# A fused attention and gate network on one core: the raw logits change PSUM banks, and the steps get a new order

## The chip, the cores and the metric

One core of a Trainium2 chip runs the whole program. Its engines are TensorE (PE, with its weight loads as PEld), VectorE (DVE), ScalarE (ACT) and GpSimd (POOL); SyncE (SP) issues nearly all DMAs. The metric is the device time of one execution in microseconds, as the median of several runs.

## The reference, cut to what matters

The input is x, 16 batches of 512 tokens with 256 features, layer-normalised to xn. Two networks read xn and their results are multiplied:

```
s = talking_heads_attention(xn)      # 16 heads of 16; logits mixed over heads before and
                                     # after the softmax
g = silu(local_gate(xn))             # 2 layers: windowed attention with 8 heads of 64,
                                     # window 128, then layernorm, gated gelu MLP
out = x + s * g

logits = einsum('bhid,bhjd->bhij', q, k) * SCALE     # the "raw" logits
logits = einsum('bhij,gh->bgij', logits, Wpre)       # the "mixed" logits
attn   = softmax(logits)
attn   = einsum('bhij,gh->bgij', attn, Wpost)
out    = einsum('bhij,bhjd->bhid', attn, v)
```

All of it is float32; the products of the gate are split in a high and a low part (three matmuls for one).

## The kernel before, in words

The program is a list of steps. `program()` (L242) strings together `AHEAD` (work for batch 0), then for each batch the text `ORDER` (L126; `FIRST_ORDER` and `LAST_ORDER` for the first and last), and each engine walks through that one list in `Counts.run` (L561), doing its own part of each step and waiting on semaphores for the others. Every engine therefore works strictly in the written order: an instruction that waits holds all that is written behind it on its engine.

Two strands share the list. The **talking-heads strand** goes, per batch:

- `raw.n.c` (32 a batch: 4 query tiles n, 8 pairs of heads c). TensorE multiplies queries by keys, one matmul into each of two banks (L963). ACT copies both banks to `raw_sb` (L1282), which has two slots and waits for the DMA of two steps before. SP waits for both copies and stores the slot in `raw_all` in DRAM (L714). The last c of a tile also issues the loads of the next queries.
- `scores.m` (32 a batch). TensorE mixes the heads of 16 query rows, read back through `raw_mix` (3 slots), into S0 and S1 (L975). DVE takes the maximum of each bank (L1547) and ACT the exponential (L1290). SP then loads a later `raw_mix`.
- `mixers.m`, `mix.m`, `values.c`, `project.t`: row sums inverted, the second mixing into M0 and M1, copies by ACT and DVE (`store_mixed`, L583), the product with the values and the output projection.
- `talk_q`, `talk_k`, `talk_v`: the projections of the next batch, in S0 and S1.

The **gate strand** goes, twice a batch: `x_turn`, `qkv` (banks F0, F1, F2), `q_turn` (F3) and `k_turn` (M1), 8 times `local_scores` (F0, F1), `weigh`, `p_turn` (F2, F3) and `local_values` (M1), 4 times `out_proj` (F3), then `half_turn`, `shift_turn`, `h_turn`, six `up` with `hide`, and four `down` (F0 to F3).

PSUM has eight banks, S0, S1, M0, M1, F0 to F3, and `banks_of` (L254) says which a step fills. A counting loop over the list (L288) numbers the fillings of each bank; before a step fills a bank, TensorE waits until the bank's last filling is emptied:

```
for k in ("S0", "S1"):
    if now.was_filled(step, k):
        pe.wait_ge(emptied[k], now.fill(step, k) - 1)
```

In the kernel before, `raw`, `scores` and the three `talk` steps all use S0 and S1. The steps `w_1_hi`, `w_1_lo`, `w_2_lo`, `w_o_lo`, `qkv_hi`, `qkv_lo`, `heads_v`, `ropes` and `keys` are loads by SP alone.

Of the kernel before, what the change touches and what calls it, by code (L numbers as in the profile page):

```python
# [131 lines left out]
mix.4 weigh.0.3 sigmoid.3 local_values.0.1 p_turn.0.2 mixers.6 silu gated qkv_hi.1 scores.7 mix.5 local_scores.0.5
weigh.0.4 out_proj.0.0 local_values.0.2 raw.2.1 mixers.7 p_turn.0.3 store local_scores.0.6 weigh.0.5 mix.6 scores.8
local_values.0.3 weigh.0.6 p_turn.0.4 raw.2.2 mixers.8 mix.7 raw.2.3 out_proj.0.1 local_values.0.4 w_1_hi.0 p_turn.0.5
raw.2.4 local_scores.0.7 local_values.0.5 values.1 p_turn.0.6 weigh.0.7 scores.9 mix.8 out_proj.0.2 local_values.0.6
raw.2.5 p_turn.0.7 raw.2.6 local_values.0.7 mixers.9 scores.10 out_proj.0.3 mix.9 half_turn.0 mixers.10 scores.11
# [5 lines left out]
join.1.3 q_turn.1.2 raw.3.6 k_turn.1.2 x_turn.0 ropes mix.16 scores.18 q_turn.1.3 k_turn.1.3 mixers.17 mixers.18
project.1 talk_k local_scores.1.0 scores.19 mix.17 local_scores.1.1 scores.20 weigh.1.0 mix.18 weigh.1.1 mixers.19
raw.3.7 split_k local_scores.1.2 w_o_lo.0 mix.19 p_turn.1.0 local_scores.1.3 weigh.1.2 weigh.1.3 keys talk_q
p_turn.1.1 local_values.1.0 w_1_hi.1 values.4 mixers.20 local_values.1.1 scores.21 p_turn.1.2 mix.20 mixers.21
local_scores.1.4 scores.22 out_proj.1.0 weigh.1.4 local_values.1.2 split_q p_turn.1.3 mixers.22 scores.23 mix.21
local_scores.1.5 mix.22 mixers.23 weigh.1.5 p_turn.1.4 local_values.1.3 scores.24 local_scores.1.6 mix.23 out_proj.1.1
scores.25 weigh.1.6 p_turn.1.5 local_values.1.4 values.5 mixers.24 local_values.1.5 raw.0.0 mixers.25 local_scores.1.7
scores.26 mix.24 out_proj.1.2 weigh.1.7 raw.0.1 p_turn.1.6 raw.0.2 mix.25 raw.0.3 p_turn.1.7 local_values.1.6
scores.27 local_values.1.7 project.2 raw.0.4 mixers.26 out_proj.1.3 raw.0.5 w_1_lo.1 mixers.27 mix.26 half_turn.1  # L150
scores.28 shift_turn.1 mix.27 raw.0.6 raw.0.7 h_scale.1 values.6 mixers.28 scores.29 h_turn.1 scores.30 mixers.29
# [7 lines left out]
k_turn.0.1 raw.1.2 bound mixers.1 join.0.2 qkv.0.3 sigmoid.0 mix.0 raw.1.3 scores.2 q_turn.0.2 join.0.3 k_turn.0.2
raw.1.4 q_turn.0.3 k_turn.0.3 raw.1.5 mixers.2 mix.1 raw.1.6 local_scores.0.0 scores.3 weigh.0.0 local_scores.0.1  # L160
mix.2 scores.4 mixers.3 p_turn.0.0 raw.1.7 sigmoid.1 weigh.0.1 mixers.4 local_scores.0.2 scores.5 mix.3
local_scores.0.3 p_turn.0.1 sigmoid.2 weigh.0.2 local_values.0.0 values.0 raw.2.0 mixers.5 local_scores.0.4 scores.6
mix.4 weigh.0.3 sigmoid.3 local_values.0.1 p_turn.0.2 mixers.6 silu gated qkv_hi.1 scores.7 mix.5 local_scores.0.5
weigh.0.4 out_proj.0.0 local_values.0.2 raw.2.1 mixers.7 p_turn.0.3 store local_scores.0.6 weigh.0.5 mix.6 scores.8
local_values.0.3 weigh.0.6 p_turn.0.4 raw.2.2 mixers.8 mix.7 raw.2.3 out_proj.0.1 local_values.0.4 w_1_hi.0 p_turn.0.5
raw.2.4 local_scores.0.7 local_values.0.5 values.1 p_turn.0.6 weigh.0.7 scores.9 mix.8 out_proj.0.2 local_values.0.6
raw.2.5 p_turn.0.7 raw.2.6 local_values.0.7 mixers.9 scores.10 out_proj.0.3 mix.9 half_turn.0 mixers.10 scores.11
w_1_lo.0 shift_turn.0 mixers.11 mix.10 w_2_lo.0 scores.12 raw.2.7 h_scale.0 mix.11 h_turn.0 mixers.12 scores.13
project.0 up.0.0 up.0.1 raw.3.0 hide.0.0 hide.0.1 up.0.2 up.0.3 hide.0.2 hide.0.3 mixers.13 up.0.4 raw.3.1 up.0.5
raw.3.2 hide.0.5 hide.0.4 values.2 norm raw.3.3 mix.12 scores.14 scale mix.13 qkv_lo.0 down.0.0 down.0.1 scores.15  # L170
down.0.2 mixers.14 down.0.3 raw.3.4 x_turn.1 mix.14 mixers.15 scores.16 qkv.1.0 join.1.0 mix.15 qkv.1.1 mixers.16
scores.17 q_turn.1.0 k_turn.1.0 join.1.1 qkv.1.2 q_turn.1.1 k_turn.1.1 raw.3.5 join.1.2 qkv.1.3 heads_v values.3
join.1.3 q_turn.1.2 raw.3.6 k_turn.1.2 x_turn.0 ropes mix.16 scores.18 q_turn.1.3 k_turn.1.3 mixers.17 mixers.18
# [1845 lines left out]
```

## Time and profile before

| | us |
|---|---|
| median of 3 runs | 5281.58 |
| lowest and highest | 5248.23 and 5287.87 |
| the profiled execution | 5270.36 |
| span of its instructions | 5268.6 |
| busy: PE, PEld | 4501.8 (85%), 3376.1 (64%) |
| busy: ACT, DVE, POOL | 3361.2 (64%), 3139.3 (60%), 1772.8 (34%) |
| mean granted TensorE clock | 0.940 |
| DMA, share of 16 engines | 55.2% on SP's queue |

PE is busy when any matmul is in flight. The granted clock is 1 at 2.4 GHz and 0.5 at 1.2 GHz; a mean between the two is a mixture of stretches at either level. Idle time is put down to the engine and line whose semaphore ended it; "issue" means that nothing in the profile ended it. A batch starts about every 320 us from the second one on.

### The profile page before, as it was taken

How to read it: one execution, taken by the hardware profiler on the slowest of the kernel's cores; microseconds unless marked ns; L12 is line 12 of the kernel's file. 1: busy time of each engine (PE TensorE's matmuls, PEld its weight loads, DVE VectorE, ACT ScalarE, POOL GpSimd, SP SyncE). 2: the span in 40 equal slices, each digit the busy share in tenths (PEclk: the TensorE clock that was granted, in tenths of full speed). 3: DMA queues.
4: the chain of work that ended last, by engine and by line, in shares of the span. 5: the costliest groups of instructions: out<-in, count | busy, mean ns of one | idle time of the engine just before them, and what ended most of it. 6: DMA issues, size and time to landing. Idle time of an engine off the chain costs nothing. (4 is left out here: it accounts for less than half of the span.)

```text
span 5268.6 us, 184953 instructions
## 1 busy us (share of the span) xinstructions
PE 4501.8 (85%) x75160; PEld 3376.1 (64%) x75160; DVE 3139.3 (60%) x8220; ACT 3361.2 (64%) x8621; POOL 1772.8 (34%) x1069
## 2 busy tenths in 40 slices
PE   3888888889988888888889888888888889888897
PEld 2666666666666666666666666666666666666665
DVE  3566556665556665656666566655566656566565
ACT  2666667666666665666666676666666666666665
POOL 2232333433324342333423333333243423334232
PEclk7998999999999999999999999999999999999999
DMA  6555566655566565566555665655665555655552
GB/s 195 206 178 206 186 189 204 184 189 192 192 208 190 187 192 184 188 194 214 171 204 190 193 206 177 201 187 187 209 188 199 182 200 181 201 203 169 194 173 81
DMA packets 397527, 997.62 MB, mean 189 GB/s; under 512 B 36496, under 2 KB 103056, under 8 KB 395152
## 3 DMA queue, kind: packets, MB, share of 16 engines
q1 hardware_dynamic: 385888, 969.02, 55.2%
q0 software_dynamic: 10800, 16.78, 1.6%
q8 instruction: 604, 9.90, 0.8%
q14 instruction: 235, 1.93, 0.1%
HBM read 655.35 MB, written 338.69 MB: 189 GB/s over the span
## 5 line engine op out<-in xcount | busy, mean ns | idle before, releaser
L1302 ACT ACTIVATE probs<-bank_S,neg_max 128x512 f32<-128x512 f32 x1024 | 692.4, 681 | 588.6 <-DVE neg_max L1554 563.7
L1003 PEld LDWEIGHTS bank_M<-mixer_n,probs 64*64 64x64 f32 x32768 | 626.6, 145 | 300.6 <-issue 276.3
L1554 DVE TENSOR_REDUCE neg_max<-bank_S 128x1 f32<-128x512 f32 x1024 | 658.0, 684 | 252.9 <-PE bank_S L986 248.7
L1855 POOL TENSOR_TENSOR l_probs<-l_probs,l_inv 128x1024 f32<-128x1024 f32 (+1 forms) x256 | 428.7, 1680 | 1089.5 <-DVE l_inv L1661 1089.5
L1003 PE MATMUL bank_M<-mixer_n,probs 64*64 64x64 f32 x32768 | 664.6, 232 | 112.5 <-issue 61.6
L986 PE MATMUL bank_S<-raw_mix,w_pre 64*64 64x512 f32 x4096 | 613.4, 663 | 144.6 <-ACT raw_sb L1288 66.0
L1840 POOL TENSOR_TENSOR inv_norms<-norms_c,minus_half 128x16 f32<-128x16 f32 x128 | 417.3, 3260 | 893.4 <-DVE norms_c L1595 893.4
L1288 ACT ACTIVATE raw_sb<-bank_S 128x512 f32<-128x512 f32 x1024 | 556.5, 599 | 211.5 <-PE bank_S L972 138.1
L1367 ACT ACTIVATE l_probs<-l_probs,l_least 128x256 f32<-128x256 f32 (+1 forms) x1024 | 480.6, 473 | 99.6 <-DVE l_least L1641 98.2
L1861 POOL TENSOR_TENSOR hidden_lo<-shared,hidden_hi 128x512 fp32r<-128x512 f32 x192 | 243.8, 1287 | 824.1 <-ACT hidden_hi L1438 824.1
L972 PE MATMUL bank_S<-keys,queries 48*128 48x512 f32 x1024 | 268.5, 515 | 256.0 <-ACT probs L1302 141.0
L592 DVE COPY mixed<-bank_M 128x512 f32<-128x512 f32 x512 | 348.8, 681 | 226.2 <-PE bank_M L1003 225.2
L1641 DVE CUSTOM_DVE_ANT_0 l_probs<-bank_F,mask,inv_norms 128x256 f32<-128x256 f32 (+1 forms) x1024 | 402.7, 447 | 0.7 <-issue 0.7
L1310 ACT ACTIVATE mixer_n<-mixer,row_inv 128x64 f32<-128x64 f32 x1024 | 295.6, 343 | 119.5 <-DVE row_inv L1545 119.4
L1743 DVE SCALAR_TENSOR_TENSOR shared<-bank_F,b,shared 128x512 f32<-128x512 f32 x192 | 143.8, 749 | 377.6 <-ACT shared L1432 349.7
L592 ACT COPY mixed<-bank_M 128x512 f32<-128x512 f32 x512 | 296.5, 579 | 94.7 <-PE bank_M L1003 92.7
L972 PEld LDWEIGHTS bank_S<-keys,queries 48*128 48x128 f32 x1024 | 105.4, 191 | 367.5 <-ACT probs L1302 153.0
L1581 DVE TENSOR_TENSOR shared<-bank_F,rot 128x512 f32<-128x512 f32 x512 | 321.2, 683 | 20.8 <-PE bank_F L914 19.4
L1022 PE MATMUL bank_M<-mixed,v_heads 128*32 128x64 f32 x16384 | 286.8, 229 | 49.9 <-issue 39.3
L912 PE MATMUL bank_F<-w_qkv_hi,xT_hi 128*128 128x512 f32 x768 | 314.2, 409 | 6.4 <-DVE xT_lo L1514 5.2
L1115 PE MATMUL bank_M<-pT,att 128*64 128x128 f32 x3584 | 264.1, 287 | 60.7 <-DVE mixed L592 37.6
L1022 PEld LDWEIGHTS bank_M<-mixed,v_heads 128*32 128x32 f32 x16384 | 260.0, 116 | 84.0 <-issue 69.9
(161 smaller groups left out, 10317.7 us busy)
## 6 DMA issues: line engine op xcount, KB each, us to landing
raw_all<-raw_sb SPq DMA_DIRECT2D x512, 512.0 KB, 3.5
raw_mix<-raw_all SPq DMA_DIRECT2D x512, 512.0 KB, 4.5
w_qkv_lo<-split_qkv SPq DMA_DIRECT2D x60, 768.0 KB, 6.1
w_qkv_hi<-split_qkv SPq DMA_DIRECT2D x60, 768.0 KB, 7.1
w_hi<-split SPq DMA_DIRECT2D x60, 704.0 KB, 5.0
w_lo<-split SPq DMA_DIRECT2D x60, 704.0 KB, 6.5
queries<-spilled_q SPq DMA_DIRECT2D x384, 64.0 KB
keys<-spilled_k SPq DMA_DIRECT2D x96, 256.0 KB, 7.6
```

Of the source, the lines that this page charges most:

```text
L592: copy(to, bank[k][:].rearrange("p (t c i) -> p t c i", t=2, i=HI)).then_inc(emptied[k], 1)
L972: mm(bank[f"S{hp}"][:], queries[rows, c, :], keys[rows, c, :], start=True, stop=True)\
L986: last = mm(bank[f"S{r}"][half * (P // 2):(half + 1) * (P // 2), :], w_pre[rows, :], raw_mix[rows, slot, half, :], start=True, stop=True)
L1003: last = mm(bank[f"M{r}"][keys, at:at + GH * HI], probs[rows, (2 * m + t) % PB, j * P + keys.start:j * P + keys.stop], mixer_n[rows, m % 2 ...
L1022: last = mm(bank["M0"][PAD * q:PAD * (q + 1), r * CI:(r + 1) * CI], v_heads[:, now.b % 2, j, pair:pair + PAD], mixed[:, j, g, :], start=(j ...
L1288: fn(raw_sb[:, c % SB, hp, :], bank[f"S{hp}"][:], ACT.Copy).then_inc(emptied[f"S{hp}"], 1)
L1302: fn(probs[:, n % PB, :], bank[k][:], ACT.Exp, bias=neg_max[:, n % 2:n % 2 + 1], accum_out=row_sum[:, n % 4:n % 4 + 1]).then_inc(emptied[k ...
L1367: fn(l_probs[:, u % LB, j, lo:], l_probs[:, u % LB, j, lo:], ACT.Exp, scale=-1.0, bias=l_least[:, u % 2, j:j + 1], accum_out=l_sum[:, u % ...
L1554: v.tensor_reduce(neg_max[:, t:t + 1], bank[k][:], AX.X, ALU.max, negate=True)\
L1641: ins = v.tensor_tensor_reduce(l_probs[:, u % LB, j, lo:], bank[k][:, pair * 2 * P + lo:(pair + 1) * 2 * P], mask[:, lo:], inv_norms[:, t, ...
L1840: g.tensor_tensor(inv_norms[:, t, :], norms_c[:], minus_half[:], ALU.pow).then_inc(inv_norm_done, 1)
L1855: g.tensor_tensor(l_probs[:, u % LB, :, lo:], l_probs[:, u % LB, :, lo:], l_inv[:, u % 2, :, None].to_broadcast([P, 4, 2 * P - lo]), ALU.m ...
```

## The change

The step `raw` gets the banks F2 and F3 in place of S0 and S1; all waits, copies and the matmul's target follow. `scores` keeps S0 and S1. The three order texts are replaced by new ones with the same steps. No instruction's shape, no buffer in SBUF and no DMA changes.

```
 def banks_of(step):
     kind = step[0]
-    if kind in ("raw", "scores"):
+    if kind == "raw":
+        return ["F2", "F3"]
+    if kind == "scores":
         return ["S0", "S1"]
...
             def keys_in(step):      # and the same in split_q
-                    sp.wait_ge(filled["S1"], now.fill(("raw", TW - 1, HC8 - 1), "S1", ago=1))
+                    sp.wait_ge(filled["F3"], now.fill(("raw", TW - 1, HC8 - 1), "F3", ago=1))
...
             def raw(step, n, c):    # SP
-                for k in ("S0", "S1"):
+                for k in banks_of(step):
                     sp.wait_ge(emptied[k], now.fill(step, k))
...
             def raw(step, n, c):    # TensorE
-                for k in ("S0", "S1"):
+                for k in banks_of(step):
                     if now.was_filled(step, k):
                         pe.wait_ge(emptied[k], now.fill(step, k) - 1)
                 for hp in range(HP):
                     rows = slice(hp * SEEN, hp * SEEN + STACK)
-                    mm(bank[f"S{hp}"][:], queries[rows, c, :], keys[rows, c, :], start=True, stop=True)\
-                        .then_inc(filled[f"S{hp}"], 1)
+                    mm(bank[f"F{2 + hp}"][:], queries[rows, c, :], keys[rows, c, :], start=True, stop=True)\
+                        .then_inc(filled[f"F{2 + hp}"], 1)
...
             def raw(step, n, c):    # ACT
-                    act.wait_ge(filled[f"S{hp}"], now.fill(step, f"S{hp}"))
-                    fn(raw_sb[:, c % SB, hp, :], bank[f"S{hp}"][:], ACT.Copy).then_inc(emptied[f"S{hp}"], 1)
+                    act.wait_ge(filled[f"F{2 + hp}"], now.fill(step, f"F{2 + hp}"))
+                    fn(raw_sb[:, c % SB, hp, :], bank[f"F{2 + hp}"][:], ACT.Copy).then_inc(emptied[f"F{2 + hp}"], 1)
```

The order, cut to four pieces of `ORDER` (old above new): the first windows of layer 0, the scaling of its hidden layer, the start of layer 1, and the `up` steps of layer 1.

```
-scores.0 qkv.0.0 join.0.0 scores.1 qkv.0.1 join.0.1 mixers.0 q_turn.0.0 k_turn.0.0 raw.1.0 qkv.0.2 raw.1.1 q_turn.0.1
-k_turn.0.1 raw.1.2 bound mixers.1 join.0.2 qkv.0.3 sigmoid.0 mix.0 raw.1.3 scores.2 q_turn.0.2 join.0.3 k_turn.0.2
+scores.0 raw.1.0 qkv.0.0 mixers.0 join.0.0 scores.1 raw.1.1 qkv.0.1 k_turn.0.0 q_turn.0.0 scores.2 join.0.1 raw.1.2
+mixers.1 mix.0 qkv.0.2 q_turn.0.1 mixers.2 k_turn.0.1 join.0.2 raw.1.3 scores.3 mix.1 raw.1.4 mixers.3 qkv.0.3
...
-w_1_lo.0 shift_turn.0 mixers.11 mix.10 w_2_lo.0 scores.12 raw.2.7 h_scale.0 mix.11 h_turn.0 mixers.12 scores.13
+out_proj.0.2 local_values.0.6 p_turn.0.7 local_values.0.7 scores.11 out_proj.0.3 half_turn.0 raw.2.5 mixers.10
+shift_turn.0 raw.2.6 w_1_lo.0 scores.12 mixers.11 h_scale.0 w_2_lo.0 mix.10 raw.2.7 h_turn.0 mix.11 mixers.12
...
-down.0.2 mixers.14 down.0.3 raw.3.4 x_turn.1 mix.14 mixers.15 scores.16 qkv.1.0 join.1.0 mix.15 qkv.1.1 mixers.16
+down.0.3 mix.14 x_turn.1 scores.16 raw.3.1 mixers.15 qkv.1.0 join.1.0 mix.15 raw.3.2 scores.17 qkv.1.1 q_turn.1.0
...
-mixers.30 mix.28 up.1.0 up.1.1 hide.1.0 hide.1.1 scores.31 mix.29 up.1.2 hide.1.2 up.1.3 w_2_lo.1 hide.1.3 mix.30
-mixers.31 up.1.4 up.1.5 mix.31 talk_v hide.1.5 qkv_lo.1 hide.1.4 values.7 down.1.0 project.3 down.1.1 down.1.2
+scores.30 h_turn.1 mixers.30 mix.29 scores.31 up.1.0 hide.1.0 up.1.1 mix.30 mixers.31 hide.1.1 up.1.2 up.1.3 mix.31
+hide.1.2 qkv_hi.0 hide.1.3 up.1.4 up.1.5 hide.1.5 hide.1.4 values.7 qkv_lo.1 project.3 down.1.0 down.1.1 down.1.2
```

## Rows read from the trace of the kernel before

**Rows 1.** Busy time and clock in three stretches: setup, batch 0, the rest.
```profile
core 0: us, PE busy (x) PEld busy (x) DVE busy (x) ACT busy (x) POOL busy (x), PEclk, DMA share, GB/s
0.00:102.00 102.00, 19.11 (x72) 13.17 (x72) 26.54 (x36) 20.26 (x28) 23.01 (x17) 0.65 0.67 212
102.00:461.00 359.00, 301.69 (x4784) 228.09 (x4788) 203.40 (x518) 219.52 (x545) 105.40 (x63) 0.92 0.56 191
461.00:5264.00 4803.00, 4180.96 (x70308) 3134.86 (x70300) 2909.31 (x7667) 3121.45 (x8048) 1643.90 (x989) 0.95 0.58 189
```

**Rows 2.** PE's waits over the span: us in total, times, longest.
```profile
PE bank_S L972 <- ACT probs L1302: 141.0, 107, 2.8
PE bank_S L986 <- ACT raw_sb L1288: 66.0, 85, 2.9
...
PE bank_S L972 <- ACT raw_sb L1288: 60.9, 96, 1.7
PE bank_S L986 <- ACT probs L1302: 60.7, 69, 1.9
...
PE bank_M L1115 <- DVE mixed L592: 37.6, 33, 2.1
```

**Rows 3.** PE in order of time: start, length, instructions; a stretch without waits.
```profile
2307.70 1.09 PE L986 MATMUL bank_S<-raw_mix,w_pre 64*64 64x512 f32 x8
2308.72 1.09 PE L1099 MATMUL bank_F<-ident,l_probs 128*128 128x128 f32 x8
2309.75 1.09 PE L1115 MATMUL bank_M<-pT,att 128*64 128x128 f32 x16
```

**Rows 4.** In order of time, the last scaling of a batch: two raw steps.
```profile
2338.06 0.49 PE L972 MATMUL bank_S<-keys,queries 48*128 48x512 f32 x2 [0.35 <-ACT probs L1302]
...
2338.62 1.08 ACT L1288 ACTIVATE raw_sb<-bank_S 128x512 f32<-128x512 f32 x2 [0.23 <-PE bank_S L972]
...
2339.85 0.50 PE L972 MATMUL bank_S<-keys,queries 48*128 48x512 f32 x2 [1.30 <-ACT raw_sb L1288]
...
2341.20 1.09 ACT L1288 ACTIVATE raw_sb<-bank_S 128x512 f32<-128x512 f32 x2 [1.50 <-DMA raw_all<-raw_sb]
...
2344.57 0.65 PE L1022 MATMUL bank_M<-mixed,v_heads 128*32 128x64 f32 x13 [1.71 <-issue]
...
2345.14 1.98 PE L986 MATMUL bank_S<-raw_mix,w_pre 64*64 64x512 f32 x8
```

**Rows 5.** In order of time: scores.12 is evicted, raw.2.7 waits for it.
```profile
2173.31 1.28 DVE L1554 TENSOR_REDUCE neg_max<-bank_S 128x1 f32<-128x512 f32 x2
...
2174.70 0.68 ACT L1302 ACTIVATE probs<-bank_S,neg_max 128x512 f32<-128x512 f32 x1
...
2175.61 0.50 PE L972 MATMUL bank_S<-keys,queries 48*128 48x512 f32 x2 [2.75 <-ACT probs L1302]
```

**Rows 6.** In order of time: qkv.0.1 ends; ACT's copy of F2; the next raw.
```profile
2077.85 0.39 PE L914 MATMUL bank_F<-w_qkv_hi,xT_lo 128*128 128x512 f32 x1
...
2079.91 0.59 ACT L1345 ACTIVATE att<-bank_F 128x512 f32<-128x512 f32 x1
...
2080.26 0.51 PE L972 MATMUL bank_S<-keys,queries 48*128 48x512 f32 x2
2080.69 0.50 PE L912 MATMUL bank_F<-w_qkv_hi,xT_hi 128*128 128x512 f32 x1
```

**Rows 7.** Groups: line, op, count, then busy, mean ns, idle before, what ended it.
```profile
L1376 ACT ACTIVATE pT<-bank_F 128x512 f32<-128x512 f32 (+1 forms) x256 | 138.5, 541 | 54.0 <-PE bank_M L1115 31.2 <-PE bank_F L1099 22.4
L1353 ACT ACTIVATE att<-bank_F 128x512 f32<-128x512 f32 x128 | 77.1, 603 | 0.0
L1302 ACT ACT_TABLE_LOAD x47 | 60.3, 1283 | 0.8
L1861 POOL TENSOR_TENSOR hidden_lo<-shared,hidden_hi 128x512 fp32r<-128x512 f32 x192 | 243.8, 1287 | 824.1 <-ACT hidden_hi L1438 824.1
```

**Rows 8.** The waits of SP's own queue: us in total, times, longest.
```profile
SPq L720 <- ACT raw_sb L1288: 1856.4, 562, 12.6
```

More of the change, by code:

```diff
@@ L132 @@
[L132 to L136, printed above, removed]
@@ L142 @@
[L142 to L146, printed above, removed]
@@ L147 @@
[L147 to L151, printed above, removed]
@@ new lines @@
+down.0.3 mix.14 x_turn.1 scores.16 raw.3.1 mixers.15 qkv.1.0 join.1.0 mix.15 raw.3.2 scores.17 qkv.1.1 q_turn.1.0
+mixers.16 values.3 mixers.17 join.1.1 k_turn.1.0 raw.3.3 qkv.1.2 q_turn.1.1 mix.16 scores.18 join.1.2 raw.3.4
+mixers.18 k_turn.1.1 qkv.1.3 join.1.3 q_turn.1.2 k_turn.1.2 raw.3.5 x_turn.0 q_turn.1.3 heads_v ropes mix.17 scores.19
+k_turn.1.3 project.1 raw.3.6 mixers.19 local_scores.1.0 mix.18 raw.3.7 local_scores.1.1 weigh.1.0 weigh.1.1 talk_k
+local_scores.1.2 p_turn.1.0 mix.19 scores.20 w_o_lo.0 weigh.1.2 local_scores.1.3 p_turn.1.1 local_values.1.0 talk_q
@@ L159 @@
[L159 to L173, printed above, removed]
@@ L184 @@
-mixers.31 up.1.4 up.1.5 mix.31 talk_v hide.1.5 qkv_lo.1 hide.1.4 values.7 down.1.0 project.3 down.1.1 down.1.2
-qkv_hi.0 down.1.3 w_o_lo.1
+scores.0 raw.1.0 qkv.0.0 mixers.0 join.0.0 scores.1 raw.1.1 qkv.0.1 k_turn.0.0 q_turn.0.0 scores.2 join.0.1 raw.1.2
+mixers.1 mix.0 qkv.0.2 q_turn.0.1 mixers.2 k_turn.0.1 join.0.2 raw.1.3 scores.3 mix.1 raw.1.4 mixers.3 qkv.0.3
+k_turn.0.2 join.0.3 q_turn.0.2 raw.1.5 mix.2 q_turn.0.3 bound scores.4 k_turn.0.3 raw.1.6 local_scores.0.0 mixers.4
+sigmoid.0 mix.3 raw.1.7 weigh.0.0 w_1_hi.0 local_scores.0.1 scores.5 p_turn.0.0 weigh.0.1 local_scores.0.2 sigmoid.1
@@ new lines @@
+out_proj.0.2 local_values.0.6 p_turn.0.7 local_values.0.7 scores.11 out_proj.0.3 half_turn.0 raw.2.5 mixers.10
+shift_turn.0 raw.2.6 w_1_lo.0 scores.12 mixers.11 h_scale.0 w_2_lo.0 mix.10 raw.2.7 h_turn.0 mix.11 mixers.12
+scores.13 up.0.0 hide.0.0 up.0.1 hide.0.1 mixers.13 values.2 up.0.2 up.0.3 hide.0.2 hide.0.3 up.0.4 up.0.5 hide.0.5
+hide.0.4 qkv_hi.1 mix.12 norm scores.14 scale qkv_lo.0 raw.3.0 mix.13 down.0.0 down.0.1 mixers.14 scores.15 down.0.2
+down.0.3 mix.14 x_turn.1 scores.16 raw.3.1 mixers.15 qkv.1.0 join.1.0 mix.15 raw.3.2 scores.17 qkv.1.1 q_turn.1.0
@@ new lines @@
+mixers.16 values.3 mixers.17 join.1.1 k_turn.1.0 raw.3.3 qkv.1.2 q_turn.1.1 mix.16 scores.18 join.1.2 raw.3.4
+mixers.18 k_turn.1.1 qkv.1.3 join.1.3 q_turn.1.2 k_turn.1.2 raw.3.5 x_turn.0 q_turn.1.3 heads_v ropes mix.17 scores.19
+k_turn.1.3 project.1 raw.3.6 mixers.19 local_scores.1.0 mix.18 raw.3.7 local_scores.1.1 weigh.1.0 weigh.1.1 talk_k
+local_scores.1.2 p_turn.1.0 mix.19 scores.20 w_o_lo.0 weigh.1.2 local_scores.1.3 p_turn.1.1 local_values.1.0 talk_q
+mixers.20 local_scores.1.4 local_values.1.1 values.4 scores.21 mix.20 p_turn.1.2 mixers.21 weigh.1.3 split_k scores.22
@@ new lines @@
+out_proj.0.2 local_values.0.6 p_turn.0.7 local_values.0.7 scores.11 out_proj.0.3 half_turn.0 raw.2.5 mixers.10
+shift_turn.0 raw.2.6 w_1_lo.0 scores.12 mixers.11 h_scale.0 w_2_lo.0 mix.10 raw.2.7 h_turn.0 mix.11 mixers.12
+scores.13 up.0.0 hide.0.0 up.0.1 hide.0.1 mixers.13 values.2 up.0.2 up.0.3 hide.0.2 hide.0.3 up.0.4 up.0.5 hide.0.5
+hide.0.4 qkv_hi.1 mix.12 scores.14 qkv_lo.0 raw.3.0 mix.13 down.0.0 down.0.1 mixers.14 scores.15 down.0.2 down.0.3
+mix.14 x_turn.1 scores.16 raw.3.1 mixers.15 qkv.1.0 join.1.0 mix.15 raw.3.2 scores.17 qkv.1.1 q_turn.1.0 mixers.16
@@ L217 @@
+mix.28 w_2_lo.1 scores.30 h_turn.1 mixers.30 mix.29 scores.31 up.1.0 hide.1.0 up.1.1 mix.30 mixers.31 hide.1.1 up.1.2
+up.1.3 mix.31 hide.1.2 hide.1.3 up.1.4 up.1.5 hide.1.5 hide.1.4 values.7 qkv_lo.1 project.3 down.1.0 down.1.1 down.1.2
+down.1.3 w_o_lo.1 end.bound end.sigmoid.0 end.sigmoid.1 end.sigmoid.2 end.sigmoid.3 end.silu end.gated end.store
 """
```

98 lines of the change are left out of this document (51 added, 47 removed).

## The prediction, made before the changed kernel ran

> **What bounds the kernel now.** I read three views in this order: busy time by stretch, the waits of TensorE, and the order of time around its gaps. After setup TensorE is busy 4180.96 of 4803 us and 301.69 of 359 us in batch 0 [rows 1], so it is idle for 622 + 57 = 679 us; ACT and DVE stand at 65% and 61% of the 4803 us. TensorE's written order is the path, lengthened by two things. One is waiting for a bank: the four rows between raw and scores, all on S0 and S1, come to 141.0 + 66.0 + 60.9 + 60.7 = 328.6 us [rows 2], 20.5 us for each of 16 batches and nearly half of the idle time. The other is the clock. It is 0.95 in the long stretch, 0.92 in batch 0 and 0.65 in setup [rows 1], so 240 + 29 us of full-speed time are lost in the batches, 0.40 us for each idle us. The two hang together: in rows 4 TensorE waits 0.35 us, 1.30 us and 1.71 us within 7 us, and the next scores step takes 1.98 us at the 1.2 GHz level, against 1.09 us at 2.4 GHz [rows 3, 4].
>
> **How I measure a wait.** A step waits if the eviction of the bank's last filling takes longer (L) than the TensorE work written between the two (D). Step lengths come from one start to the next: scores 1.02, p_turn 1.03 [rows 3], raw 0.43 [rows 6]. L for scores is two maxima, then the last exponential: scores.12 started to be read at 2173.31 and was free at 2175.38 [rows 5], 2.1 us, with the semaphores some 2.3. L for raw: TensorE ends at 2338.55, the copies at 2339.70 [rows 4], 1.15 us. Summed pair by pair along the old text this gives 16.5 us a batch on S0 and S1, where the trace has 20.5; what it misses (ACT or DVE still busy with something else, the DMA of raw_sb, which held the copy for 1.50 us in rows 4) I cover by the factor 1.24.
>
> **The change, part by part, for one batch.**
>
> *S0 and S1 are relieved.* The old text fills the pair 67 times, 33 of them with D under 2.4 us, 20 under 1.2. The new one fills it 35 times; five have D of 1.8 to 2.3 (before talk_q, talk_v and three scores) and none is closer. They cost 1.5 us, 2.0 with the factor. Of 20.5 us, 18.5 go.
>
> *F2 and F3 are loaded.* Their fillings go from 52 to 84, those with D under 1.2 us from 5 to 29. A raw behind q_turn or qkv is the worst: raw.1.5 stands right behind q_turn.0.2, raw.1.3 and raw.3.5 one short step behind, raw.1.1, raw.1.3, raw.3.2 and raw.3.5 some 1.0 us behind a qkv. L for q_turn is one copy, 0.603 us alone [rows 7]; for qkv's F2 it was 2080.50 - 2078.24 = 2.3 us, since the copy stands behind two squares in ACT's order [rows 6]. With L of 1.2 and 1.5 these pairs make 4.2 us. Behind p_turn (0.541 us on ACT [rows 7]; raw.0.3 with nothing between) it is 1.0 us, raw behind raw 1.0, h_turn.0 right behind raw.2.7 0.6, raw behind out_proj 0.5, and the gate's steps behind raw 0.8. Together 8.1 us, 10 with the factor. From below: with every eviction at one copy (0.6) only the pairs closer than that count, about 3 us. From above: the 29 close pairs all at the 2.3 us of rows 6, with D some 0.9 on average, would be 29 x 1.4 = 40 us. I take 10, because what is waited for here is one or two plain copies, and so the raw row (1.15 us) is nearest; for the range I use 3 to 20, the upper end being half of those pairs at that 2.3 us.
>
> *Other waits move.* mix to local_values on M1 has D of 0, 0.4, 0.4 where it was 0, 1.0, 1.0 (the row now costs 37.6 us in all [rows 2]): +1.2. One local_values now follows another's filling at once: +0.9. values to mix: +0.5. No mix is closer to the last than 1.45 us, where the old text had 0.8, 1.0 and 1.2: -1. project.3 stands right behind values.7, half_turn.0 right behind out_proj.0.3: +0.5 each. x_turn.1 to qkv.1.0 loses 0.6 us of cover. The last up and the first down lie 3.3 and 3.5 us apart after 5.6 and 6.0; the last piece of that chain is POOL's 1.287 us [rows 7] behind gelu, product and copy, so about +0.5 for each layer. Sum +4. k_turn and mix change their distances on M1 both ways; 0, between -1.5 and +1.5.
>
> *ACT's tables.* The old text switches between exponential and gelu six times a batch, since scores.31 stands among the up steps and another scores run ends them; the new one four times. That is 32 loads of 1.283 us fewer [rows 7], 41 us of ACT. I cost it at nothing: an up step is twelve wide matmuls, in which ACT has one gelu and one copy to do, and no wait of up for ACT is among TensorE's large rows [rows 2]. If that cover failed, the 41 us would be the gain. The Trainium skill (ScalarE: Activation LUTs, What ACT_TABLE_LOAD costs) puts a drain of 1380 ns on top of each load; by it 85 us of ACT time would go, and the trace has no row for the drain.
>
> *SP's queue.* The order of its 32 raw stores and 32 raw_mix loads shifts with the text. SP sat 1856.4 us waiting for ACT's copy before a store [rows 8]; behind such a wait stand raw_mix, weights and queries. raw_mix for a new tile is still asked for 0.7 to 2.8 us of TensorE work after the tile's last raw, or later; for the next batch's first tile it is 0 after 1.9, with all the up and down steps as cover. talk_v moves from the end of the batch to its last third, so the loads of w_qkv_hi behind it gain some 50 us of room. 0.
>
> **Sum.** 16 x (-18.5 + 10 + 4) = -72 us of waiting. At 0.40 us of clock for each idle us, another -29 us. That makes -101 us against the profiled execution's 5270.4, or against the median 5281.6, which is 11 us higher: 5180 us.
>
> **The rivals.**
>
> *The clock doesn't follow.* The lower level came after clusters of short waits [rows 4]. The new order has shorter waits but 29 close pairs on F where S had 20 and F had 5; if their number counts and not their length, the 29 us stay: 5210 us. The Trainium skill (TensorE: Matmul & The Clock Gate, the section on PSUM-queue depth-cycling) says that micro-idles between groups of matmuls, one bank after the next, are enough for the clock to oscillate; by that rule this rival would hold, and the trace agrees that short waits suffice. For my forecast speaks that the worst clusters (raw.2.7 with 2.75 us [rows 5], raw.0.6, raw.0.7) stand where the gate's banks are idle. Chance 0.14.
>
> *The waits only move house.* If F2 and F3 cost 15 us a batch, the waiting is +8 us in sum, 5290 us; at 14, 5270. Chance 0.22.
>
> *Slower: the gate convoys behind raw.* In the eight qkv windows ACT has two squares, the F2 copy, the q_turn copy and now raw's two copies in one line, and each raw holds TensorE until its predecessor on F2 or F3 is out. qkv, q_turn and p_turn then start late, and with them the long chain over DVE and POOL. At 20 us a batch the sum is 16 x (-18.5 + 20 + 4) x 1.40 = +123 us, 5405 us. It decides from about 17 us a batch. Against it: S0 and S1 no longer hold ACT for the same pairs. Chance 0.13.
>
> *More than forecast.* F2 and F3 at the lower bound, 3 us a batch: 16 x (-11.5) x 1.40 = -258 us, 5024 us. Chance 0.13 for anything under 5110.
>
> **How the numbers follow.** The forecast (F2 and F3 at 8 to 12 us a batch, 5135 to 5225) has 0.38. Faster by over 1% is under 5229, about the least that a measurement of this kernel tells from no change; slower is over 5334. Faster: 0.38 + 0.13 + 0.09 of the clock's 0.14 = 0.60. Same: 0.05 + 0.22 = 0.27. Slower: 0.13. The range of 5085 to 5335 leaves out most of the two outer cases, 0.2 together.
>
> **What would show it.** After the change: the rows of scores behind raw, and of raw behind probs, are gone; scores behind probs at 20 to 40 us in the whole span; new rows of raw behind att, pT and raw_sb on bank_F that sum to about 160 us; mean clock 0.945 to 0.95; 64 table loads besides the first, where there were 96. It is wrong if the bank_F waits pass 270 us (then rival two or three), if "POOL" or "DVE" rows of k_turn, p_turn and down grow by more than 60 us (a chain I called covered), or if the idle time falls and the clock stays at 0.940.

## The result: 0.5% slower, and where the time went

The changed kernel took 5298.18 us (median of 20 runs, 5288.59 to 5313.67), the kernel before 5275.34 us beside it (20 runs, 5248.23 to 5300.65). The ratio is 1.0052, with a 95% interval from 1.0039 to 1.0065. The forecast was 5180 us, and a gain of over 1% had a chance of 0.6. What came lies inside the range and in "within 1%", but on the wrong side of zero. Profiles are of one execution each, and among executions of one kernel the times differ by some 0.5 to 1%, so spans and busy times carry that much noise. In the profiles "after" and "before" stand for 5300.5 and 5270.4 us, near the medians.

**The sum first.** This is the top of the page of the changed kernel (its line numbers are one higher than before):

```profile
span 5298.7 us, 184921 instructions
...
PE 4437.6 (84%) x75160; PEld 3297.3 (62%) x75160; DVE 3145.6 (59%) x8220; ACT 3339.8 (63%) x8589; POOL 1764.5 (33%) x1069
```

TensorE does the same 75160 matmuls. Span less busy time is its idle time: 5268.6 - 4501.8 = 766.8 us before, 5298.7 - 4437.6 = 861.1 us now. So there are 94 us more of waiting and 64 us less of work, +30 us together. The forecast had -72 and -29. The work became shorter, and the mean clock was higher (0.951 after 0.940). The three stretches, to be laid beside [rows 1], show that all of it lies in the batches:

```profile
core 0: us, PE busy (x) PEld busy (x) DVE busy (x) ACT busy (x) POOL busy (x), PEclk, DMA share, GB/s
0.00:102.00 102.00, 19.80 (x72) 13.65 (x72) 26.19 (x36) 20.25 (x28) 23.03 (x17) 0.66 0.67 210
102.00:461.00 359.00, 298.33 (x4800) 224.47 (x4801) 204.06 (x521) 219.79 (x549) 104.61 (x63) 0.94 0.57 194
461.00:5294.00 4833.00, 4119.51 (x70290) 3059.22 (x70288) 2915.38 (x7664) 3099.71 (x8014) 1636.10 (x989) 0.96 0.57 188
```

**Then the waits.** TensorE's waits in the changed kernel, to be laid beside [rows 2] (us in total, times, longest):

```profile
PE bank_F L973 <- issue: 93.9, 13, 10.0
...
PE bank_F L973 <- DMA keys<-spilled_k: 72.5, 4, 50.7
PE bank_F L973 <- ACT raw_sb L1289: 53.8, 76, 1.4
...
PE bank_F L973 <- ACT att L1354: 49.4, 48, 1.5
PE bank_M L1116 <- DVE mixed L593: 28.3, 39, 1.8
PE bank_M L1116 <- DVE o_locT_lo L1668: 26.8, 17, 1.6
PE bank_F L1160 <- ACT raw_sb L1289: 26.4, 8, 5.0
...
PE bank_F L1160 <- DVE shared L1713: 22.5, 8, 2.8
PE bank_M L1031 <- ACT oT L1325: 22.1, 16, 1.4
PE bank_F L973 <- ACT pT L1377: 21.3, 29, 1.0
PE bank_F L913 <- ACT raw_sb L1289: 21.2, 31, 1.2
PE bank_F L1100 <- ACT raw_sb L1289: 21.1, 17, 2.1
PE bank_F L1100 <- POOL l_probs L1856: 20.8, 15, 1.7
...
PE bank_S L987 <- ACT probs L1303: 14.9, 25, 0.7
```

Of the four large rows of S0 and S1 [rows 2] one is left, at 14.9 us. The banks F2 and F3 took over less than that. What the prediction did not have at all is the top: 13 waits of up to 10.0 us, marked "issue", and 4 for the DMA of keys. Of the latter, 50.7 us is one wait in setup, which the kernel before has too (51.0 us). Of the others, 15 stand in front of raw.0.0, the first raw step for the next batch: one in each of 15 batches, 5.5 to 10.0 us long, 114 us in all (the sixteenth, of 2 us, stands elsewhere).

**What those waits are.** "Issue" says only that the profile saw no releaser. The order of time says more. First SP's own queue in the kernel before, in the batch whose raw.0.0 starts at 2631.7 us (start, time of issuing, what is loaded or stored, how many):

```profile
2598.91 4.69 SPq L679 DMA_DIRECT2D keys<-spilled_k  x6
...
2610.17 1.27 SPq L695 DMA_DIRECT2D spilled_q<-q_hi  x2
...
2620.84 3.79 SPq L687 DMA_DIRECT2D queries<-spilled_q  x6
```

The same queue in the changed kernel, same batch (the view cuts off the first of the six loads of queries, issued at 2617.16 us):

```profile
2617.78 3.73 SPq L688 DMA_DIRECT2D queries<-spilled_q  x5
2621.60 4.88 SPq L680 DMA_DIRECT2D keys<-spilled_k  x6
```

And TensorE there, then all engines between the first load of keys and raw.0.0 (columns as in the three stretches):

```profile
2636.02 0.80 PE L973 MATMUL bank_F<-keys,queries 48*128 48x512 f32 x2 [7.48 <-issue]
2636.75 1.97 PE L1116 MATMUL bank_M<-pT,att 128*64 128x128 f32 x16
```

```profile
2621.60:2636.00 14.40, 5.45 (x218) 4.75 (x217) 3.36 (x10) 3.23 (x10) 1.89 (x1) 0.78 1.00 172
```

Before, keys was asked for 32.8 us ahead of raw.0.0 and was there long before it was needed. Now it is asked for 14.4 us ahead, behind the queries and so behind the spill of q that these wait for, and raw.0.0 starts 7.48 us late. The six loads of 256 KB land one after another, some 2 us apart, and the last one 14.3 us after the first was issued. SP needs only 4.88 us to issue them. The DMA engines are busy throughout (share 1.00) and move 172 GB/s meanwhile, so it is they that set the 14 us, in the kernel before too (share 0.94, 176 GB/s). In all 15 batches raw.0.0 starts 0.09 us after the last of the six has landed. keys was moved in the text from behind weigh.1.3 to behind local_scores.1.6, and split_k from ahead of p_turn.1.0 to behind weigh.1.3.

### The profile page after: what moved, and what is told of

Read it like the earlier page. It is cut to its first block and busy times, and to the rows that moved or that the text cites. A ratio compares the mean times of both kernels' runs of the same rounds, so it can differ in the third digit from the quotient of the medians.

```text
span 5298.7 us, 184921 instructions
## 1 busy us (share of the span) xinstructions
PE 4437.6 (84%) x75160; PEld 3297.3 (62%) x75160; DVE 3145.6 (59%) x8220; ACT 3339.8 (63%) x8589; POOL 1764.5 (33%) x1069
## 5 line engine op out<-in xcount | busy, mean ns | idle before, releaser
L1004 PEld LDWEIGHTS bank_M<-mixer_n,probs 64*64 64x64 f32 x32768 | 586.7, 141 | 248.7 <-issue 239.5
L1289 ACT ACTIVATE raw_sb<-bank_F 128x512 f32<-128x512 f32 x1024 | 555.7, 599 | 278.9 <-PE bank_F L973 265.6
L1004 PE MATMUL bank_M<-mixer_n,probs 64*64 64x64 f32 x32768 | 640.0, 227 | 104.0 <-issue 79.4
L987 PE MATMUL bank_S<-raw_mix,w_pre 64*64 64x512 f32 x4096 | 594.2, 644 | 27.5 <-ACT probs L1303 14.9
L973 PE MATMUL bank_F<-keys,queries 48*128 48x512 f32 x1024 | 265.5, 510 | 304.4 <-issue 93.9
L973 PEld LDWEIGHTS bank_F<-keys,queries 48*128 48x128 f32 x1024 | 103.8, 189 | 454.5 <-issue 287.2
L1668 DVE TENSOR_TENSOR o_locT_lo<-bank_M,o_locT_hi 128x256 fp32r<-128x256 f32 x256 | 107.9, 422 | 421.6 <-ACT o_locT_hi L1388 419.8
L1582 DVE TENSOR_TENSOR shared<-bank_F,rot 128x512 f32<-128x512 f32 x512 | 324.1, 683 | 34.9 <-PE bank_F L915 32.8
L1116 PE MATMUL bank_M<-pT,att 128*64 128x128 f32 x3584 | 268.5, 291 | 68.3 <-DVE mixed L593 28.3
L1100 PE MATMUL bank_F<-ident,l_probs 128*128 128x128 f32 x1792 | 276.7, 296 | 49.2 <-ACT raw_sb L1289 21.1
```

The costliest lines, as they stand in the source:

```text
L973: mm(bank[f"F{2 + hp}"][:], queries[rows, c, :], keys[rows, c, :], start=True, stop=True)\
L987: last = mm(bank[f"S{r}"][half * (P // 2):(half + 1) * (P // 2), :], w_pre[rows, :], raw_mix[rows, slot, half, :], start=True, stop=True)
L1004: last = mm(bank[f"M{r}"][keys, at:at + GH * HI], probs[rows, (2 * m + t) % PB, j * P + keys.start:j * P + keys.stop], mixer_n[rows, m % 2 ...
L1289: fn(raw_sb[:, c % SB, hp, :], bank[f"F{2 + hp}"][:], ACT.Copy).then_inc(emptied[f"F{2 + hp}"], 1)
L1582: ins = v.tensor_tensor(dst[:, j, :].rearrange("p (h s d) -> p h s d", h=H, s=2), x, tab[:, None, :, :].to_broadcast([P, H, 2, HD // 2]), ...
```

## The experiments

Each time is given as its ratio to the kernel before on the same chip, with its 95% interval; "after" is the changed kernel, at 1.0052. All moves were made in the three orders alike, where these have the step.

**keys earlier (e1_keys_early).** After, with this edit:

```
-local_values.1.3 split_q mixers.23 local_scores.1.6 keys scores.24
+local_values.1.3 keys split_q mixers.23 local_scores.1.6 scores.24
```

> The changed kernel, with the step keys moved from behind local_scores.1.6 to just ahead of split_q in the order texts; nothing else. Theory A (the late keys load): the first raw of each batch waited 5.5 to 10.0 us for the keys, 114 us over 15 batches, and the keys' loads were issued 14 us ahead of it; issued some 10 us earlier, they land first, the wait goes, and with its share of the clock the time falls by 110 to 160 us against the changed kernel: 5140 to 5190 us, 0.974 to 0.984 of the kernel before. Theory B (the bank waits of F2 and F3 and the gate's data chains set the pace): the wait for the keys was slack for those chains, so most of it comes back as longer waits behind raw; 5270 to 5300 us.

5255.02 us, 0.9961 (0.9939 to 0.9982). That is between the two theories. The wait for keys is gone, but only half of the 114 us came back: the span is 53 us shorter. SP now issues keys ahead of the queries, which come later in their turn, and the gaps in front of values grew from 50.8 us:

```profile
PE bank_M L1023 <- issue: 71.2, 39, 5.5
...
PE bank_F L973 <- DMA queries<-spilled_q: 23.2, 12, 3.5
```

Here keys goes out 23 to 27 us ahead of raw.0.0, and in 14 of the 15 batches within 0.3 us of the landing of the last store of spilled_k: once keys stands early, it is that store that holds it.

**keys late in the old order (e4_keys_late_in_old).** The opposite test: before, with one step moved.

```
-weigh.1.3 keys talk_q
+weigh.1.3 talk_q
...
-split_q p_turn.1.3 mixers.22 scores.23 mix.21
+split_q p_turn.1.3 mixers.22 scores.23 keys mix.21
```

> The kernel before, with the step keys moved behind scores.23, which leaves some 15 us of TensorE work between it and raw.0.0, as in the changed kernel; banks and all else as before. Theory A: the load takes 14 us from the first issue to the last landing whatever the order, and stalls in the old order hide part of it, so raw.0.0 waits 2 to 8 us in each of 15 batches, 30 to 120 us of idle, 1.008 to 1.03 of the kernel before. Theory B: SP reaches keys in time here and the lateness in the changed kernel came from SP's queue alone; within 0.4% of the kernel before.

5358.93 us, 1.0161 (1.0124 to 1.0198). The same row appears in a kernel in which raw still uses S0 and S1:

```profile
PE bank_S L972 <- issue: 131.4, 16, 13.2
```

So the wait belongs to the place of keys and not to the banks. By itself it costs 1.6%. The waits in front of raw.0.0, 4.2 to 13.2 us each, come to 129 us, and the idle time rose by 89 us (856.2 of a span of 5353.8).

**split_k earlier, keys late (e10_split_k_early).** After, with `split_k` ahead of `talk_q` instead of behind `weigh.1.3`.

> The kernel after with one step moved: split_k stands ahead of talk_q, while keys stays behind local_scores.1.6. Theory A (what costs 114 us is how late keys is issued; split_k only sets when its source is spilled): the keys DMA is still issued 14 to 10 us before raw.0.0, so raw.0.0 of each batch still waits 5 to 10 us, and the time stays within 0.3% of the kernel after, ratio to before 1.003 to 1.008. Rival B (the DMA is held by spill_k, which lands late because POOL does talk_q first): the wait falls by half or more and the ratio goes to 0.990 to 0.998.

5317.67 us, 1.0085 (1.0062 to 1.0108), a little above the expected 1.008. The stores of spilled_k now start some 44 us ahead of raw.0.0 instead of 34, and the wait stays:

```profile
PE bank_F L973 <- issue: 99.4, 15, 10.0
```

The stores had landed 35 to 38 us ahead of raw.0.0, and the loads were still issued only 13 to 14 us ahead of it. What is late is the asking, so rival B falls.

**Both earlier (e6_keys_and_split_early).** After, with `split_k` ahead of `talk_q` and

```
-p_turn.1.2 mixers.21 weigh.1.3 split_k scores.22
+p_turn.1.2 mixers.21 keys weigh.1.3 scores.22
```

> The changed kernel, with split_k moved ahead of talk_q (so that POOL does not do the 9 us of talk_q before it) and keys moved behind mixers.21. With keys early alone raw.0.0 still waited 23 us in all, now for the queries, which SP loads behind the keys. Theory A: keys and queries both land in time, the 23 us go, and the result is 15 to 35 us less than with keys early alone (5255 us): 5220 to 5240 us, below the kernel before by 0.7 to 1.0%. Theory B: what follows raw.0.0 is paced by instruction fetch (the 'issue' gaps grew from 160 to 205 us when the wait for the keys went), and the 23 us come back there: 5245 to 5260 us.

5205.47 us (5188.81 to 5216.86), 0.9886 (0.9860 to 0.9911): the best version, below both kernels, 1.7% under the changed one, and better than either theory had it. Against split_k earlier with keys late, which differs by the place of keys alone, it is 2.0 points: the 15 waits of 105 us are gone, the idle time is 96 us less and the busy time 30 us less. Every wait of raw.0.0 is gone; of DMA waits of raw only the one in setup is left.

```profile
PE bank_F L973 <- ACT raw_sb L1289: 53.0, 76, 1.4
PE bank_F L973 <- DMA keys<-spilled_k: 50.5, 1, 50.5
```

SP's queue shows why nothing is pushed aside: keys stands in a stretch in which TensorE waits for nothing behind it, 11 us before the stores of q (here raw.0.0 starts at 2578.1 us).

```profile
2549.56 3.79 SPq L680 DMA_DIRECT2D keys<-spilled_k  x6
2560.96 1.27 SPq L696 DMA_DIRECT2D spilled_q<-q_hi  x2
...
2569.66 3.78 SPq L688 DMA_DIRECT2D queries<-spilled_q  x6
```

**The banks alone (e2_banks_only).** Before, in its old order, with raw in F2 and F3:

```
+    if kind == "raw":
+        return ["F2", "F3"]
...
-                    mm(bank[f"S{hp}"][:], queries[rows, c, :], keys[rows, c, :], start=True, stop=True)\
+                    mm(bank[f"F{2 + hp}"][:], queries[rows, c, :], keys[rows, c, :], start=True, stop=True)\
```

> Raw in F2 and F3, with the order texts of the kernel before. Keys are loaded early here. 38 of the 84 fillings of F2 and F3 then stand within 1.2 us of TensorE work behind the last, where the changed kernel has 29. Theory A: banks without a new order cost more on F than they save on S, some 28 us a batch against 20.5, so 1.02 to 1.04 of the kernel before, and the order was needed. Theory B, the banks do the good and the order does the harm: 0.98 to 0.99 of the kernel before.

5740.15 us, 1.0876 (1.0839 to 1.0914). The direction was expected, the size was not: a loss of 9% where 2 to 4% were written. In this kernel line numbers are two higher than before.

```profile
PE bank_F L974 <- ACT att L1355: 135.6, 80, 4.5
PE bank_F L974 <- ACT pT L1378: 79.7, 74, 2.5
...
PE bank_F L914 <- ACT raw_sb L1290: 60.3, 47, 1.6
...
PE bank_F L974 <- DVE shared L1745: 55.3, 32, 1.8
```

The old text puts raw in the midst of qkv, p_turn and up. The new order is what makes the banks usable at all; which of its moves do it was not separated. The order alone, with raw on S0 and S1, wasn't tried, so the shares of banks and order in what is gained are not known.

**raw.2.7 behind h_turn (e5_keys_early_raw27).** The longest waits on F in the changed kernel are those of h_turn, up to 5.0 us (L1160 above). In order of time, in the place of [rows 5]:

```profile
2172.54 0.51 PE L973 MATMUL bank_F<-keys,queries 48*128 48x512 f32 x2
2172.76 0.69 ACT L1303 ACTIVATE probs<-bank_S,neg_max 128x512 f32<-128x512 f32 x1 [2.52 <-DVE neg_max L1555]
...
2173.35 1.36 DVE L1713 TENSOR_SCALAR shared<-bank_F,mean_var,rstd 128x128 f32<-128x128 f32 x4
...
2175.04 1.09 ACT L1289 ACTIVATE raw_sb<-bank_F 128x512 f32<-128x512 f32 x2
...
2175.79 1.09 PE L1160 MATMUL bank_F<-ident,shared 128*128 128x128 f32 x4 [2.75 <-ACT raw_sb L1289]
```

raw.2.7 has filled its banks at 2173.05 us. ACT first does the exponentials of scores.12, the mixer's scaling and a copy of mixed, and reads the first bank from 2175.04 to about 2175.6: L is 2.6 us, not the 1.15 of [rows 4]. Over all raw steps of this kernel the time from the second matmul's end to the second copy's end is 1.42 us in the median and over 2.7 in a quarter of them; before it was 1.18 and, at the upper quartile, 1.51. The edit, on top of keys early:

```
-raw.2.7 h_turn.0 mix.11 mixers.12
+h_turn.0 mix.11 raw.2.7 mixers.12
```

> As the kernel with keys early, and raw.2.7 moved from just ahead of h_turn.0 to behind mix.11, so that h_turn.0 does not fill F2 and F3 right behind it. h_turn.0 waited 26 us in the changed kernel for the copies of raw.2.7 and 22.5 us for the scaled hidden layer. Theory A (banks): the 26 us go, less what raw.2.7 now waits behind h_turn; 10 to 25 us less than the kernel with keys early. Theory B (the chain over DVE is what ends the wait either way): the wait stays as one for the scaled layer, within 8 us of that kernel.

5255.26 us, 0.9972 (0.9950 to 0.9993), no different from the kernel with keys early. h_turn waits as long as ever, now without raw in front of it:

```profile
PE bank_F L1160 <- issue: 53.5, 17, 3.2
```

With keys early alone L1160 had 25.2 us behind DVE's shared and 22.1 behind raw_sb, 47.3 together. Rival theory B holds. Of these 17 waits, 16 end 0.10 us after the last operation of h_scale on DVE (which stands behind the maxima of scores.12), though the profile names no releaser. The bank's path and that of h_scale end about together, so taking away one gains nothing.

**raw spread out (e7_raw_spread) and a part of it (e11_raw_spread_batch_start).** Both build on the best version and put raw steps further behind the step that filled F2 and F3 before them. In both:

```
-raw.1.3 scores.3 mix.1 raw.1.4 mixers.3 qkv.0.3
+scores.3 raw.1.3 mix.1 mixers.3 raw.1.4 qkv.0.3
...
-q_turn.0.2 raw.1.5 mix.2 q_turn.0.3 bound scores.4 k_turn.0.3 raw.1.6 local_scores.0.0
+q_turn.0.2 mix.2 q_turn.0.3 bound scores.4 k_turn.0.3 raw.1.5 local_scores.0.0
```

(raw.1.6 and raw.1.7 follow one place later.) e7_raw_spread also moves raw.3.5, raw.0.3 and local_values.1.3.

> As the kernel with keys and split_k early; moreover raw.1.3 to raw.1.7 and raw.3.5 are moved so that none stands within one short step behind q_turn, raw.0.3 comes behind local_values.1.7, and local_values.1.3 no longer follows local_values.1.2 directly. Theory A (bank waits of F2, F3 and M1 cost what they show): raw behind q_turn's copy (49 us over the span) falls to under 20, local_values behind o_locT_lo (27 us) to under 8, and the time falls by 30 to 60 us against that kernel. Theory B: such waits only move to the next step of the gate's chain; within 10 us of it.

> The best version so far (split_k ahead of talk_q, keys behind mixers.21, which stood at 0.989 of before) with only the first of the moves of raw_spread: raw.1.3 to raw.1.7 of the batch's start stand one or two steps later. Theory A (those moves carried raw_spread's loss: a later raw.1.7 puts the chain of raw_sb behind it late): the rows of raw behind raw_sb come to 100 us or more, and the ratio is above 1.005. Rival B (the loss came from the other moves, local_values.1.3, raw.3.5 and raw.0.3): the ratio stays at 0.985 to 0.995 and raw behind raw_sb near 53 us.

5339.11 us, 1.0150 (1.0124 to 1.0176), and 5303.65 us, 1.0057 (1.0039 to 1.0075). First the waits of the larger edit, then those of the smaller:

```profile
PE bank_F L973 <- ACT raw_sb L1289: 131.6, 107, 3.0
```

```profile
PE bank_F L973 <- ACT raw_sb L1289: 134.6, 110, 3.0
...
PE bank_F L973 <- ACT att L1354: 20.4, 17, 1.5
```

Neither theory for the larger edit foresaw a loss. The wait behind att fell as meant (49.4 us to 20.4, and to 0.2 with the larger edit), and the one behind raw_sb rose by 82 us. In the smaller edit 81 us of it are two waits a batch: 3.0 us in front of raw.1.4 in all 16 batches (48 us) and 2.05 us in front of raw.1.7 (33 us). The order of time shows the first:

```profile
488.58 0.50 PE L973 MATMUL bank_F<-keys,queries 48*128 48x512 f32 x2
...
491.47 0.68 ACT L1303 ACTIVATE probs<-bank_S,neg_max 128x512 f32<-128x512 f32 x1
...
492.13 1.08 ACT L1289 ACTIVATE raw_sb<-bank_F 128x512 f32<-128x512 f32 x2
...
493.35 0.49 PE L973 MATMUL bank_F<-keys,queries 48*128 48x512 f32 x2 [3.02 <-ACT raw_sb L1289]
```

raw.1.3 now stands behind scores.3, so ACT copies it only behind the two exponentials of scores.3, which themselves wait for DVE's maxima. raw.1.4 comes one mix step later and waits. The smaller edit carries 1.7 points of the ratio and the three other moves 0.9.

**Fewer table loads in the old order (e9_old_fewer_tables).** Before, with

```
-mixers.30 mix.28 up.1.0 up.1.1 hide.1.0 hide.1.1 scores.31 mix.29 up.1.2
+mixers.30 mix.28 scores.31 mix.29 up.1.0 up.1.1 hide.1.0 hide.1.1 up.1.2
```

> The kernel before, with scores.31 and mix.29 moved ahead of up.1.0, so that ACT loads its tables 64 times and not 96 (and one at the start). Theory A: the loads were covered by the up steps; within 15 us of the kernel before. Theory B: each removed load of 1.28 us is on the path of the up steps; 30 to 45 us less.

5313.23 us, 1.0089 (1.0055 to 1.0122). ACT's two groups of loads are as in the changed kernel; the first of them:

```profile
L1432 ACT ACT_TABLE_LOAD x32 | 41.1, 1283 | 0.6
```

With the 31 at L1302, 32 loads are gone and no time came back. The edit does not isolate them: the time is 48 us longer by the medians, which neither theory has. scores.31 now stands close behind scores.30, and scores behind probs went from 60.7 to 91.1 us, 30 of the 66 us by which the idle time grew. A gain from the loads could hide behind that.

**values.6 apart from mix.28 (e8_values6_earlier).** With the wait for keys gone, the largest rows left are again "issue": 87.7 us before mix and 47.5 before values in the best version. Such a gap in the changed kernel, inside values.6, where 114 of its 128 matmuls have run and no bank and no semaphore can be meant:

```profile
2669.65 0.42 PE L1023 MATMUL bank_M<-mixed,v_heads 128*32 128x64 f32 x14 [3.82 <-issue]
```

The page's list of queues has one that carries instructions (packets, MB, share of 16 engines; the 9.90 MB make 16 KB for a packet), and the changed kernel has 54 "issue" gaps of over 1 us besides those of raw.0.0. Of these, 43 end 1.15 to 1.55 us after one of its packets of 16 KB has ended, where 5% of random moments lie (from a random moment it is 4.3 us back to the last one, in the median):

```profile
q8 instruction: 604, 9.90, 0.8%
```

mix and values issue 64 and 128 small matmuls in 1.2 and 2 us. The edit, on the best version:

```
-raw.0.7 scores.29 values.6 h_scale.1 mixers.29 mix.28
+raw.0.7 values.6 scores.29 h_scale.1 mixers.29 mix.28
```

> As the kernel with keys and split_k early, and values.6 (256 matmuls and weight loads in 1.9 us) moved from behind scores.29 to ahead of it, so that 16 instead of 256 instructions stand right before mix.28 (128 instructions). Theory A (the 'issue' gaps are waits for PE's own instructions, which come in packets of 16 KB): the gaps in mix.28, 34 to 40 us in 24 places, fall below 15 us, and the time by 10 to 30 us. Theory B ('issue' in mix.28 is a wait for a semaphore that the profile doesn't name): they stay at 30 to 45 us.

5218.26 us, 0.9909 (0.9883 to 0.9936), no faster than the best version. The gaps in front of mix fell from 87.7 to 71.8 us, and scores behind probs rose from 10.4 us to 24.1:

```profile
PE bank_M L1004 <- issue: 71.8, 54, 3.7
...
PE bank_S L987 <- ACT probs L1303: 24.1, 37, 1.4
```

The sum alone says little, for in kernels in which nothing was moved near mix.28 it lies anywhere from 64.6 to 93.0 us. mix.28 by itself does: in the seven kernels of the new order with values.6 in its old place it has 32 to 40 us in 23 or 24 gaps, and here 15.7 us in 6. So what stands in front of mix.28 does set its gaps, about as theory A had it, but there was nothing to win with this step.

**The two halves side by side.** Span and busy time are from each page, idle is their difference, the clock is the mean granted one:

| kernel | span | TensorE busy | idle | clock | ratio |
|---|---|---|---|---|---|
| before | 5268.6 | 4501.8 | 766.8 | 0.940 | 1 |
| after | 5298.7 | 4437.6 | 861.1 | 0.951 | 1.0052 |
| banks alone | 5743.9 | 4647.8 | 1096.1 | 0.913 | 1.0876 |
| before, keys late | 5353.8 | 4497.6 | 856.2 | 0.933 | 1.0161 |
| after, keys early | 5245.6 | 4438.0 | 807.6 | 0.958 | 0.9961 |
| after, keys and split_k early | 5187.0 | 4414.5 | 772.5 | 0.963 | 0.9886 |
| after, split_k early, keys late | 5312.2 | 4444.0 | 868.2 | 0.950 | 1.0085 |
| the best version, raw of the batch's start spread | 5316.1 | 4494.1 | 822.0 | 0.947 | 1.0057 |

The best version's profiled execution was the fastest of its six (5188.8 us, median 5205.5), that of the last row the slowest of its eight (5317.9, median 5303.7). Their difference is thus some 30 us too large in the table.

The table also shows what the best version gains by. Its idle time is that of the kernel before (772.5 and 766.8 us), and it is TensorE's busy time that is 87 us less. Gaps without a releaser are 168 us in it, after 156 before.

## Why the prediction was wrong, step by step

The forecast of TensorE's idle time was 16 x (-18.5 + 10 + 4) = -72 us. It came out at +94, which is 166 us off. Term by term:

| step | forecast | measured |
|---|---|---|
| S0 and S1 relieved | -296 | -305 |
| F2 and F3 loaded | +160 | +211 |
| other waits | +64 | +74 (the rest) |
| SP's queue | 0 | +114 |
| clock (busy time) | -29 | -64 |

*SP's queue: "0".* **This is the step that failed.** It priced raw_mix and the weights behind talk_v, and it never followed the move of keys, though the order texts show it. In its place the runs showed 15 waits of 5.5 to 10.0 us, +114 us. The numbers were there: in the kernel before, the last keys had landed some 14 us after the first was issued, and issue stood 32 to 38 us ahead of raw.0.0. In the new text only some 15 us of TensorE work (an estimate from the steps' lengths) lie between keys and raw.0.0, and SP comes to it behind the queries, 13 to 15 us ahead. Keys late in the old order (+1.6%), keys early in the new one (-0.9 points), keys and split_k early (-1.7) and split_k alone (no gain) show it from all sides. With keys and split_k in better places the change is a gain of 1.1%, where 1.9% was forecast.

That this comes so near is partly luck. Without the 114 us the forecast of idle time would still have been off by 52 us (-20 against -72), and in the best version the idle time is 6 us above the kernel before. The rest of the gain is busy time, 87 us less, where 29 were forecast.

*S0 and S1 are relieved.* Right. The four rows of 328.6 us [rows 2] came down to 14.9 us of scores behind probs, with another 9.1 us of talk_q and talk_v behind probs: -305 us, where 296 were forecast.

*F2 and F3 are loaded: 10 us a batch.* It was 211 / 16 = 13.2, inside the range of 3 to 20 and near the 14 of the rival "the waits only move house". By kind, forecast (with the factor 1.24) against measured, in us a batch: raw behind qkv or q_turn 5.2 and 3.3 (49.4 + 2.7 us); behind p_turn 1.2 and 1.3; behind out_proj 0.6 and 0.6; raw behind raw 1.2 and 3.4 (53.8 us); h_turn behind raw.2.7 0.7 and 1.7 (26.4 us); the gate's other steps behind raw 1.0 and 3.0 (21.2 + 21.1 + 5.8 us). The pairs that I called the worst were dearer on paper than on the chip; their L of 1.2 and 1.5 us stands in no row. The pairs in which raw's own copy is what has to end were mis-sized by a factor of 2.7 in sum. Its L of 1.15 us came from a place where ACT was free [rows 4]; behind scores it is 2.6 us, as the order of time around h_turn shows. The row that had warned of this was the same raw.2.7 with its 2.75 us [rows 5]: in this batch the wait has moved from raw to h_turn and has kept its length.

*Other waits: 4 us a batch.* As the rest of the sum it is 4.6, so the size is right, in part by luck: the places are only half so. project behind oT (22.1 us) and down behind hidden_lo (12.1) were named. M1's wait behind mixed did not grow, it fell from 37.6 to 28.3; o_locT_lo (26.8 us after 7.3), p_turn behind l_probs (20.8) and h_turn behind shared (22.5) weren't named, and mix behind att (25.3 us) and talk_k behind w_v_lo (27.5), which went away, weren't either.

*ACT's tables: 0.* Not contradicted, and not isolated. There are 64 loads beside the first, as forecast, and the loads taken out of the old order gave nothing back, but another wait rose with the same edit. The Trainium skill (ScalarE: Activation LUTs, What ACT_TABLE_LOAD costs) adds a drain of 1380 ns to each load. The trace does not agree: in both kernels ACT stands idle for 18 ns ahead of a load and for 12 ns behind it, in the median, and the gelu behind it takes 688 ns, as any other.

*The clock: 0.40 us for each idle us.* Wrong as a rule, though the sign came out. Idle time rose by 94 us and the busy time of the same matmuls fell by 64. Four pairs of rows in the table show how little one rate fits. Keys late in the old order adds 89 us of idle time and no busy time (4497.6 for 4501.8). Keys late in the new one, with split_k early in both, adds 96 us of idle time and 30 us of busy time. Keys early alone takes 53 us of idle time and no busy time (4438.0 for 4437.6). The spread raws add 50 us of idle time and 80 us of busy time (less some noise, see above). A long wait isn't free of clock either: in the changed kernel the clock was at its lower level at the end of every one of the 15 waits of raw.0.0 and stayed there for 3.4 to 6.7 us of work. In the rows above, the local_values step behind raw.0.0 takes 1.97 us, against 1.09 at the upper level [rows 3]. In the old order such stretches took the place of others: 498 us of its work after setup ran at the lower level, and 494 with keys late. So what a wait costs in clock depends on where it stands; by which property of the place, its length or the waits around it, no run here separates.

The rival "the clock doesn't follow" falls too. Behind it stood a rule of the Trainium skill (TensorE: Matmul & The Clock Gate, PSUM-queue depth-cycling), that the engine's micro-idles between groups of matmuls can come often enough to make the clock oscillate. The spread raws agree with it: their added waits are of 2 and 3 us. What the rival made of it, that 29 close pairs on F would keep the clock down, did not come: TensorE's waits of 0.5 to 1 us rose from 165 to 262 in number, those of 1.5 to 3 us fell from 113 to 78, and the mean clock rose to 0.951.

*The other rivals.* "Slower: the gate convoys behind raw" has the sign and not the mechanism: it needed 17 us a batch on F and 5334 us or more. "The waits only move house" (5270 to 5290) is the nearest in time. In cause it is half right: F2 and F3 took over 13.2 of the 19.0 us a batch that S0 and S1 gave up, and in the best version the idle time is indeed that of before, but that kernel is faster by its clock, which this rival did not have. No case had a late load in it.

*What should have shown it.* All the tripwires stayed silent: F at 211 us (wrong from 270), scores behind probs at 14.9 (below the 20 to 40 forecast), chains of k_turn, p_turn and down 35 us longer (wrong from 60). Idle time that falls with a constant clock did not occur, but idle time that rises did, and no tripwire was set for a row that isn't in the profile of before.

## What to carry to other kernels

When steps move, list for each load that a moved step issues the time from issue to landing of the whole group and the work left between issue and use, in the new text, and read what the queue has to pass first; that is the same count of L and D as for banks, and here it was worth more than the error on the banks (114 us against 51). Take L from where the evicting engine stands in its own order at that place, not from a place where it was free. A bank that is moved wants the order moved with it: the same banks were worth +8.8% in the old order and are part of -1.1% in the repaired new one.
